# Per-head sums of squares of the delta-rule outputs: taken by ScalarE's accumulator in four operations instead of by a VectorE reduction

## What is computed

```
o = gated_delta_rule(q, k, v, g, beta)                  # (b, t, 32 heads, 96)
gate = (h @ Wg).reshape(b, t, H, DV)
o = rmsnorm(o, gnorm_w) * silu(gate)                    # mean of o*o over the 96 elements of a head
o = o.reshape(b, t, VD) @ Wo
```

## Time and profile before

| | |
|---|---|
| time, median of 3 runs | 2382.16 us (2377.2 to 2392.59) |
| the profiled execution's own time | 2376.38 us |
| its span | 2374.4 us |
| mean granted TensorE clock | 0.957 of full |
| PE busy | 2167.4 us (91%) |
| PEld busy | 1721.6 us (73%) |
| DVE busy | 1801.3 us (76%) |
| ACT busy | 1196.1 us (50%) |
| POOL busy | 1420.4 us (60%) |

### The profile page before, as it was taken

How to read it: one execution, slowest core, us unless ns; L and a number is a source line. 1 busy time by engine, 2 the same in 40 slices (tenths; PEclk the granted TensorE clock), 3 DMA queues, 4 the chain that set the end, 5 groups by cost and what they waited for, 6 DMA issues and landing times. The chain is left out here.

```text
span 2374.4 us, 50717 instructions
## 1 busy us (share of the span) xinstructions
PE 2167.4 (91%) x17776; PEld 1721.6 (73%) x17776; DVE 1801.3 (76%) x3955; ACT 1196.1 (50%) x3011; POOL 1420.4 (60%) x2176
## 2 busy tenths in 40 slices
PE   6489999999999999999999999999999998799997
PEld 2367777777777777777777777777777776455665
DVE  5678888888888888888888888888888885145544
ACT  4245555555555555555555555555555554222221
POOL 2567777777777777777777777777777774000000
PEclk9789999999999999999999999999999997799998
DMA  4211221112111211222112212212121110401100
GB/s 134 64 35 37 39 61 35 36 39 59 36 40 36 59 39 37 39 57 39 39 36 59 39 36 39 60 36 39 36 59 37 39 28 2 135 1 36 36 10 9
DMA packets 203838, 102.82 MB, mean 43 GB/s; under 512 B 97010, under 2 KB 185147, under 8 KB 203587
## 3 DMA queue, kind: packets, MB, share of 16 engines
q1 hardware_dynamic: 203266, 99.46, 18.5%
q10 hardware_dynamic: 320, 0.13, 0.0%
HBM read 69.69 MB, written 2.54 MB: 30 GB/s over the span
## 5 line engine op out<-in xcount | busy, mean ns | idle before, releaser
L911 DVE SCALAR_TENSOR_TENSOR dr_y<-dr_ps,cw,dr_y 128x255 f32<-128x255 f32 (+2 forms) x1152 | 476.1, 473 | 137.2 <-ACT dr_y L1044 137.2
L772 PE MATMUL dr_ps<-dr_w,dr_am 128*128 128x96 f32 x3072 | 438.0, 288 | 22.4 <-ACT dr_w L1096 22.4
L772 PEld LDWEIGHTS dr_ps<-dr_w,dr_am 128*128 128x128 f32 x3072 | 396.2, 198 | 57.5 <-ACT dr_w L1096 46.7
L1096 ACT COPY dr_w<-dr_ps 128x384 f32<-128x384 f32 x384 | 184.3, 480 | 292.0 <-PE dr_ps L772 292.0
L1044 ACT ACTIVATE dr_y<-dr_ps,cw 128x256 f32<-128x256 f32 x384 | 160.9, 470 | 138.8 <-PE dr_ps L704 137.2
L1194 POOL TENSOR_TENSOR dr_fo<-dr_vo,dr_nhalf 128x4 f32<-128x4 f32 x128 | 129.5, 1012 | 149.7 <-DVE dr_vo L982 145.0
L704 PE MATMUL dr_ps<-hT,wqk 128*128 128x256 f32 x768 | 195.5, 392 | 20.8 <-PEq L145 20.8
L955 DVE TENSOR_TENSOR dr_am<-dr_ps,dr_dec 128x512 f32<-128x512 f32 x256 | 164.9, 686 | 61.5 <-PE dr_ps L755 59.8
L1160 POOL TENSOR_TENSOR dr_dg<-const,dr_gam 128x512 f32<-128x512 f32 x128 | 130.3, 1039 | 126.5 <-DVE dr_gam L947 126.5
L838 PE MATMUL dr_ps<-wo,dr_oT 128*128 128x256 f32 x768 | 199.2, 397 | 1.1 <-ACT dr_oT L1132 1.0
L755 PE MATMUL dr_ps<-dr_qk 64*128 64x256 f32 x1024 | 161.2, 437 | 42.1 <-DVE dr_y L911 29.1
(11 more groups left out here) (219 smaller groups left out, 4814.9 us busy)
## 6 DMA issues: line engine op xcount, KB each, us to landing
dr_abc<-scr_a SPq DMA_DIRECT2D x64, 512.0 KB, 5.4
dr_qk<-dr_sy SPq DMA_DIRECT2D x384, 48.0 KB, 2.0
dr_bcb<-scr_b SPq DMA_DIRECT2D x128, 64.0 KB, 4.8
dr_c<-dr_b SPq DMA_DIRECT2D x512, 4.0 KB, 1.8
dr_qk<-dr_sy SPq DMA_DIRECT2D x128, 32.0 KB, 1.9
ex_modb<-scr_mod SPq DMA_DIRECT2D x4, 1024.0 KB, 8.0
wv<-in_Wv SPq DMA_DIRECT2D x8, 384.0 KB, 3.5
wo<-in_Wo SPq DMA_DIRECT2D x1, 3072.0 KB, 12.0
```

What stands on the lines that cost most here:

```text
L772: last = pe.matmul(ps[:, bank, h * DV:(h + 1) * DV], wt(h), x[:, h * DV:(h + 1) * DV], start=(start and h == 0), stop=(h == QH - 1), skip_ ...
L911: v.scalar_tensor_tensor(y[:, slot, x:T], ps[:, BANK[n], off:off + T - x], cw[:, t, TAPS - 1 - x:TAPS - x], y[:, slot, x:T], ALU.mult, ALU ...
L1096: act.copy(w[:, c, :], ps[:, CW, 0:QV]).then_inc(s["w_ok"], 1)
```

## The change

ACT squares the outputs of each head by an operation of its own (four of 128x96 instead of one of 128x384), and each also writes the sum of its squares to one column of `mso` by the accumulator output. Every one of the four raises `sqo_ok`, so DVE waits for four counts per chunk. DVE's `tensor_reduce`, and the wait for its result, are left out, and so is the semaphore `mso_ok`. ACT gets one wait more before its squares: `vo_ok` of the chunk before, so that `mso` isn't overwritten before L982 has read it.

```diff
             def mean(st, c):
                 it, m = st
                 n = it * CH + c
-                v.wait_ge(s["sqo_ok"], n + 1)
-                v.tensor_reduce(mso[:], sqo[:].rearrange("p (h d) -> p h d", h=QH), AX_X, ALU.add).then_inc(s["mso_ok"], 1)
-                v.wait_ge(s["mso_ok"], n + 1)
+                v.wait_ge(s["sqo_ok"], (n + 1) * QH)
                 v.scalar_tensor_tensor(vo[:], mso[:], 1.0 / DV, e2[:, m, c * QH:(c + 1) * QH], ALU.mult,
                                        ALU.add).then_inc(s["vo_ok"], 1)
...
             def squares(st, c):
                 it, m = st
                 act.wait_ge(s["o_ps"], it * CH + c + 1)
-                act.activation(sqo[:], ps[:, CO, 0:QV], ACT.Square).then_inc(s["sqo_ok"], 1)
+                wait(act, s["vo_ok"], it * CH + c)
+                for h in range(QH):
+                    hs = slice(h * DV, (h + 1) * DV)
+                    act.activation(sqo[:, hs], ps[:, CO, hs], ACT.Square, accum_out=mso[:, h:h + 1]).then_inc(s["sqo_ok"], 1)
```

More of the change, by code:

```diff
@@ L510, in delta_rule @@
             c_st bc_ps ab_ok xs xb_ok c32_ok c32t_ok te_ok b32_ok n1_ps n2_ps wn_ok cn_ok
-            w0_ps res_ps d_ps s_ps ks_ps o_ps ot_ps wo_ps w_ok rs_ok S_ok r1_ok r1h_ok sqo_ok mso_ok vo_ok fo_ok
+            w0_ps res_ps d_ps s_ps ks_ps o_ps ot_ps wo_ps w_ok rs_ok S_ok r1_ok r1h_ok sqo_ok vo_ok fo_ok
             og_ok oT_ok acc_ok""".split()
```

## The result

The changed kernel takes 2445.14 us (median, 2439.7 to 2449.91) against 2387.09 us for the kernel before beside it: a ratio of 1.026, 95% interval 1.0223 to 1.0296. It is slower by some 58 us. The profiled execution took 2448.27 us, with a span of 2446.2 us.

What follows compares the result with a forecast made beforehand. PE was taken to set the pace, waiting on a chain through ACT's full block and DVE's taps. 2376.4 + 37.8 (ACT's delay) + 48 (clock) = 2462.2, with 5.8 for the median 2468 us; range 2412 to 2515.

Steps and rivals of the forecast that it cites:

- The chain of a turn: Across the loop's turn: PE's chunk 1 outputs, ACT's full block, DVE's taps, PE's scores at L755; the turn grows 0.59 us.
- ACT's delay: At chunk 1's squares on ACT: four square-and-read pairs delay the block by 0.59 us a turn, 37.8 us over 64 steps.
- Chunk 0 is covered: At chunk 0's squares: ACT's 1.27 us of idle time before L1126 takes the delay, so it costs nothing.
- DVE's saving buys nothing: On DVE: dropping reduction and wait frees 0.58 us per chunk, 74 us in all, but nothing is counted for it.
- L720 takes the wait: On PE at the norms (L720): the wait grows from 0.18 to 0.77 us; L755's wait stays at 0.6.
- Clock: At PE's emptiest stretch around L720: more waiting brings 20 more clock falls at 2.40 us each, 48 us.
- The added wait: On ACT before its squares: `vo` of the chunk before comes some 12 or 13 us ahead, so the wait costs nothing.

Runs made afterwards that it cites:

- the moved cast: ACT's cast of the values (L1086) moved behind the third projection's eviction: 2447.19 us in the changed kernel, 2367.0 us in the kernel before.
- chunk 0 alone: Kernel before with only chunk 0's squares taken per head; chunk 1 keeps one operation and DVE's reduction: 2373.73 us, ratio 0.998.
- the kernels with products: Kernel before and changed kernel, each with one or two additional unused 128x256 products on PE; one made the kernel before 1.5% faster.
- the chunk 1 kernel: Kernel before with only chunk 1's squares taken per head; chunk 0 keeps one operation and DVE's reduction: 2438.73 us, ratio 1.0255.
- the one with the additional square: Kernel before with one more 128x512 ACT square, never read and without accumulator, ahead of chunk 1's squares: 2445.47 us, ratio 1.0291.

## Why the prediction was right, and where it was off

Predicted were 2468 us, range 2412 to 2515; measured 2445.14, inside, slower with 0.90 on that side. Step by step:

- *The chain of a turn* (PE's outputs of chunk 1, ACT's block, taps, scores, all the rest PE) was right: clean turns grew by what the block grew, in three kernels. But the taps aren't the block's only way to PE: it holds PE at L720, where all of the growth showed, and, as the moved cast brought out, by its next operation (L1026) at L772.
- *ACT's delay*, 0.59 us x 64 = 37.8 us forecast: 0.54 in the turn, 34 us over the 63 turns. A pair takes 0.22 to 0.24 us instead of 0.245: the read starts 0.13 to 0.15 us behind its square.
- *Chunk 0 is covered*: right, shown by chunk 0 alone.
- *DVE's saving buys nothing*: right, shown by the kernel without the reduction. The Trainium skill (VectorE: DVE Perf Modes, Rules for kernel authors), which the prediction weighed, gives its advice on `tensor_reduce` for the hot path. This one is off the path. At 0.54 us it isn't slower than its neighbours of 384 columns, and taking it out gains nothing. A size was wrong: I forecast some 2.7 us of waiting ahead of the taps, and it is 2.30, because `vo` waits for the sums and DVE isn't ahead by 0.58 us.
- *L720 takes the wait*: 0.77 forecast, 0.73 measured; at L755 0.6 and 0.63.
- *Clock*: here is the term that was mis-sized. I took 20 more falls at 2.40 us, 48 us. There were 19 more of 63, but the clock cost only some 28 us more. Of the 32 fallen turns of the first 61, 11 are of a kind that I didn't know, 1.0 to 1.3 us, and the median of all is 2.23 over a clean turn. The count came from splitting the difference between 13 and all, so its hit is luck: nothing in my reading of the trace gave it, and the kernels with products show that more waiting of PE isn't all that sets it. With 28 for 48 and 34 for 37.8 the sum is 2376.4 + 62 = 2438, plus 5.8 for the median of the runs then known, 2444. That this meets the 2445.14 is in part luck too: the profiled execution took 2448.27, with 8.9 us at the loop's start that no term has.
- *The added wait*: it can't be told apart from zero; the chunk 1 kernel has it, the one with the additional square doesn't, and both turns grew as their blocks did.

The three runs that stood under the prediction had a median of 2382.16; in later comparisons the kernel before came to 2387.09, 2378.94, 2379.58 and 2373.73. This is a spread of 0.6%. Among its executions the one of 2367.44 us had a mean granted clock of 0.955 and the one of 2389.47 us 0.948. Of the kernel before only one was kept as a trace, so whether other turns fall in the longer ones isn't shown.

## What to carry to other kernels

An engine at 50% can still hold the path, if its operations stand back to back between two waits of the engine that bounds; look for the block, not for the share, before moving work onto it. Splitting one ScalarE operation into n with accumulator outputs costs a start for each and a read for each: it does no harm where the engine idles behind, as in chunk 0, and even there it won nothing. Where PE has little to do for some microseconds, waiting added there can cost twice, as here, 34 us by itself and some 28 by the clock, and work put there can be better than free. It need not be: try it in the very kernel. And when an operation is moved out of the way, look what stands behind its new place: here it was the next cast that PE needs.

## What the runs showed of the hardware

- An accumulator output is a second ScalarE instruction of 0.19 to 0.22 us; in a row of 128x96 squares from PSUM it adds 0.09 us per square (0.35 us for four), and a square with its read takes 0.22 us from start to start.
- The clock's fall comes in three lengths here, by the time at the lower level: 6.8 us (a mean of 0.89 for the turn, mostly 2.2 to 2.4 us lost), 3.4 us (0.94 to 0.95, 1.0 to 1.3 us lost) and 10.2 us (0.85, 4.0 to 4.15 us lost). In the first 61 turns all 13 of the kernel before were of the first kind, 11 of 32 in the changed kernel of the second, and with two products all were of the second. The third came six times without the reduction, four times in the changed kernel with the cast moved, and once in the changed kernel with one product.
- One product of 128x256 that nobody reads, 0.5 us of PE in each turn, made the kernel before 36 us faster.
